# Ranking edges inside a tile by a summing comparison on VectorE: one sorting pass of a graph kernel, rebuilt

## The reference

```
# layer 0
att   = sigmoid(concat(h[src], rel[type]) @ att_w + att_b)      # one gate an edge
aggr  = segment_sum(att * h[dst], src)                          # by source node
x     = x + tanh(aggr @ W_w.T + W_b)
# layer 1: keys, values from h[dst], queries from h[src], weights from the attributes;
alpha = segment_softmax(sum(queries[src] * keys), src)
x     = x + lin(ssp(lin(h) + segment_sum(alpha * messages, src)))
```

## Time and profile before

| | |
|---|---|
| median of three runs | 7741.46 us (7740.86 to 7743.12) |
| the profiled execution | 7789.98 us, its span 7787.8 us, mean clock granted to TensorE 0.611 of full speed |
| busy over the span | PE 3233.5 us (42%), PEld 2600.9 (33%), VectorE 3605.5 (46%), ScalarE 2450.0 (31%), GpSimd 3252.3 (42%) |
| DMA | 497.92 MB, mean 64 GB/s |
| setup and histogram | up to about 283 us |
| sort | about 283 to 3963 us |
| layer 0 | to about 4600 us; layer 1 to about 7560 us |

### The profile page before, as it was taken

The page is one execution under the profiler, slowest core; times in us unless marked ns, Lnnn a source line. Parts: engine busy times, 40 slices in busy tenths (PEclk is TensorE's granted clock), DMA queues, the critical chain, the costliest instruction groups (busy, mean ns, idle before and its releaser), DMA issues. The chain is left out here.

```text
span 7787.8 us, 93760 instructions
## 1 busy us (share of the span) xinstructions
PE 3233.5 (42%) x31759; PEld 2600.9 (33%) x31760; DVE 3605.5 (46%) x6570; ACT 2450.0 (31%) x5029; POOL 3252.3 (42%) x3386
## 2 busy tenths in 40 slices
PE   4744444444444444444457743332222223332224
PEld 3633443343343343344357621111111111111113
DVE  7744443443444444444367724444444444444443
ACT  0122222222232232232212234444444444444432
POOL 0144344444434434434450045555555555555542
PEclk9866666666666666666666655555555555555555
DMA  3011111111111111111156322222333333333310
GB/s 46 29 52 45 42 50 45 43 49 46 44 42 52 45 42 52 45 42 51 37 126 125 76 75 83 83 83 83 86 86 86 88 84 84 84 84 83 86 55 17
DMA packets 651114, 497.92 MB, mean 64 GB/s; under 512 B 556547, under 2 KB 565379, under 8 KB 651056
## 3 DMA queue, kind: packets, MB, share of 16 engines
q1 hardware_dynamic: 509120, 240.52, 12.6%
q0 software_dynamic: 108640, 196.86, 8.7%
q10 hardware_dynamic: 33296, 59.81, 2.2%
HBM read 286.61 MB, written 210.32 MB: 64 GB/s over the span
## 5 line engine op out<-in xcount | busy, mean ns | idle before, releaser
L518 POOL DMA_INDIRECT records<-rec,place x1612 | 1550.5, 962 | 2388.8 <-ACTq L637 1901.1
L1210 POOL DMA_INDIRECT got_a<-kv_table,idx_a x1612 | 1524.3, 946 | 1418.5 <-DVE idx_a L1322 914.3
L1225 PE MATMUL p_a<-ident,flat_attr 128*128 128x128 f32 x434 | 124.3, 434 | 1730.6 <-ACT attr_t L1266 965.6
L550 PE MATMUL p_h<-window,dst_hot 128*128 128x64 bf16 x4836 | 378.2, 218 | 943.4 <-issue 943.4
L725 DVE TENSOR_SCALAR dst_hot<-p_dst,number 128x512 bf16<-128x512 f32 x434 | 308.9, 712 | 972.6 <-remote 707.4
L539 PE MATMUL p_look<-parts,lo_hot_t 128*128 128x98 bf16 x4836 | 538.1, 250 | 468.3 <-DVE earlier L743 461.2
L743 DVE TENSOR_TENSOR earlier<-p_same,less_b 128x512 bf16<-128x512 f32 x434 | 282.5, 651 | 938.7 <-PE p_same L585 519.7
L610 ACT COPY h_dst<-p_h 128x256 f32<-128x256 f32 x434 | 155.0, 357 | 1770.7 <-remote 1291.6
L1225 PEld LDWEIGHTS p_a<-ident,flat_attr 128*128 128x128 f32 x434 | 75.2, 214 | 1768.9 <-ACT attr_t L1266 989.9
L1345 DVE TENSOR_TENSOR prod<-got_a,wide 128x1664 f32<-128x1664 f32 x62 | 117.0, 1887 | 1108.8 <-remote 1107.7
L550 PEld LDWEIGHTS p_h<-window,dst_hot 128*128 128x128 bf16 x4836 | 280.5, 114 | 954.2 <-issue 954.2
(11 more groups left out here) (339 smaller groups left out, 9872.4 us busy)
## 6 DMA issues: line engine op xcount, KB each, us to landing
sums<-packed_a ACTq DMA_DIRECT2D x62, 936.0 KB
q_starts<-zero_q SPq DMA_DIRECT2D x62, 884.0 KB
rec_r<-records SPq DMA_DIRECT2D x124, 442.0 KB
qin<-q_starts SPq DMA_DIRECT2D x62, 884.0 KB
attr_a<-records SPq DMA_DIRECT2D x62, 442.0 KB
records<-rec,place POOLq DMA_INDIRECT x1612
got_a<-kv_table,idx_a POOLq DMA_INDIRECT x1612
stage<-in_edge_attr SPq DMA_DIRECT2D x61, 416.0 KB
```

Source lines behind the costliest of these rows:

```text
L518: nc.gpsimd.indirect_dma_start(k.records, bass.IndirectOffsetOnAxis(ap=place[b][:, t:t + 1], axis=0), rec[b][:, t, :], None).then_inc(s_se ...
L550: last = nc.tensor.matmul(p_h[:, j * D:(j + 1) * D], dst_hot[qb][:, j * P:(j + 1) * P], window[b][:, part, :], start=(part == 0), stop=(pa ...
L1210: nc.gpsimd.indirect_dma_start(got[b][:, t, :], None, k.kv_table, bass.IndirectOffsetOnAxis(ap=idx[b][:, t:t + 1], axis=0)).then_inc(s_got ...
L1225: last = nc.tensor.transpose(p_a[:, g * P - c0:(g + 1) * P - c0], flat_attr[:, g * G:(g + 1) * G, :].rearrange("p t c -> p (t c)"), k.iden ...
```

## The change

**Transposed one-hots without transposes.** `setup` writes three fields of all edges (lo, hi, and destination relative to the chunk) into DRAM (`field_rows`), each chunk's edges in a row by partition. SP loads a chunk's piece, three partitions of 3328 elements in bf16 (`fields`). TensorE reads a group's columns out of it with a step of 26 elements (`rows`) and multiplies them with `select`, three constant matrices of 3 x 128, in three products of 512 columns: p_lo repeats an edge's lo on all partitions, p_src its node number, p_dst its destination. ScalarE makes the transposed one-hots from p_lo by `relu(1 - |lo - partition|)`, an Abs into `lo_away` and a Relu into `lo_hot_t`, now in fp32.

**The rank in the tile on VectorE.** For each tile one `scalar_tensor_tensor` compares p_src with the edge's own source, multiplies by `before` (an earlier edge), and sums along the row into `rank`, an accumulator output. p_same, `earlier` and their product in `look` go.

**The places on VectorE.** p_place and its bf16 parts go. `tables` holds 52 tables of 49 numbers in fp32, one for each tile of two chunks, and the logit's behind them; VectorE adds a tile's counts from p_hist to a table to get the next (`add`, four a group). `look` is one fp32 product a tile, over the tile's table and the logit's, instead of three to seven in bf16. The place is summed with `rank` once a chunk (`s_place`).

**h in one part.** p_h is one fp32 product a tile, in one of two banks, from a window of `h_table`; `h3_table` goes, and `setup` no longer makes the three parts. ScalarE's gate products read p_h itself and write `h_gated`, so `h_copy` goes. `assemble` copies `h_gated` (1664 columns) and the gates into the record, and runs inside g == 2 instead of g == 3.

```
# setup, SP: ahead of the store of h_table
+   sp.wait_ge(s_fields, 1)
+   for a, field in enumerate((k.lo_b, k.hi_b, k.dst_in)):
+       sp.dma_start(k.field_rows[a, :].rearrange("(c p t) -> p c t", p=P, t=T),
+                    field[:].rearrange("p (c t) -> p c t", t=T)).then_inc(k.s_field_rows, 16)
    sp.dma_start(by_node(k.h_table), h[:]).then_inc(s_table, 16)
-   sp.dma_start(k.h3_table...)
# setup, VectorE
-   c.then(nc.vector.tensor_copy(h3[:, :, 0, :], h[:]))
-   c.then(nc.vector.tensor_tensor(h_rest[:], h[:], h3[:, :, 0, :], ALU.subtract))
-   c.then(nc.vector.tensor_copy(h3[:, :, 1, :], h_rest[:]))
-   nc.vector.tensor_tensor(h3[:, :, 2, :], h_rest[:], h3[:, :, 1, :], ALU.subtract).then_inc(s_h3, 1)
# sort, SP
+   wait(sp, s_dst, (n - 1) * GROUPS)
+   sp.dma_start(fields[b][:], k.field_rows[:, bass.ds(n * P * T, P * T)]).then_inc(s_fields[b], 16)
    wait(sp, s_h, (n - 1) * GROUPS)
-   sp.dma_start(window[b]..., k.h3_table[bass.ds(base, P), :])
+   sp.dma_start(window[b][:], k.h_table[bass.ds(base, P), :]).then_inc(s_window[b], 16)
# sort, GpSimd
+   pool.wait_ge(s_place, n + 1)
    pool.wait_ge(s_ready, n + 1)
# sort, TensorE: look(), for the group before
-   wait(pe, s_h_copied, q)
+   pe.wait_ge(s_tables, q + 1)
+   pe.wait_ge(s_lo_hot, q + 1)
    for j in range(size(g)):
+       last = nc.tensor.matmul(both, lo_hot_t[qb][:, j * P:(j + 1) * P], k.tables[:, slot:LOGIT + 1:LOGIT - slot, :], start=True, stop=True)
    ...
+   wait(pe, s_gated, q - 1)
+       last = nc.tensor.matmul(p_h[qb][:, j * D:(j + 1) * D], dst_hot[qb][:, j * P:(j + 1) * P], window[b][:], start=True, stop=True)
# sort, TensorE: a group
+   pe.wait_ge(s_fields[b], 16 * (i + 1))        # once a chunk
+   rows = fields[b][:].rearrange("r (p t) -> r t p", t=T)[:, g * G:g * G + m, :]
+   wait(pe, s_lo_away, q)
+   nc.tensor.matmul(p_lo[:, 0:m * P], k.select[:, LO, :], rows, start=True, stop=True).then_inc(s_lo, 1)
+   wait(pe, s_ranked, q)
+   nc.tensor.matmul(p_src[:, 0:m * P], k.select[:, NODE, :], rows, start=True, stop=True).then_inc(s_src, 1)
+   wait(pe, s_dst_hot, q)
+   nc.tensor.matmul(p_dst[:, 0:m * P], k.select[:, TO, :], rows, start=True, stop=True).then_inc(s_dst, 1)
+   wait(pe, s_tables, q)
    (counts into p_hist, then look of the group before)
-   (transposes, p_dst, p_same, p_place)
# sort, ScalarE
+   nc.scalar.activation(lo_away[qb][:, 0:m * P], p_lo[:, 0:m * P], ACT.Abs, bias=k.minus_number[:]).then_inc(s_lo_away, 1)
+   act.wait_ge(s_lo_away, q + 1)
+   wait(act, s_look, q - 1)
+   nc.scalar.activation(lo_hot_t[qb][:, 0:m * P], lo_away[qb][:, 0:m * P], ACT.Relu, bias=k.ones[:, 0:1], scale=-1.0).then_inc(s_lo_hot, 1)
    (gated:)
+   nc.scalar.activation(gate[b][:, ...], logit[b][:, ...], ACT.Sigmoid).then_inc(s_gate, 1)
+   for j, t in enumerate(tiles):
+       last = nc.scalar.activation(h_gated[b][:, t, :], p_h[qb][:, j * D:(j + 1) * D], ACT.Copy, scale=gate[b][:, t:t + 1])
+   last.then_inc(s_gated, 1)
    (assemble:)
-   nc.scalar.copy(place[b][:], place_all[:, cols])
+   wait(act, s_sent[b], SCATTERED * i)
+   nc.scalar.copy(rec[b][:, :, GATE], gate[b][:])
+   nc.scalar.copy(rec[b][:, :, H0:REC], h_gated[b][:])
-   if g == 3 and not at_start(i, b):
+   if g == 2 and not at_start(i, b):
        assemble(n - 1, i - 1 + b, 1 - b)
# sort, VectorE: a group
+   c.mark(add(b, g, 0))          # tables[slot + 1] = tables[slot] + p_hist of the tile
    dst_hot
+   c.wait(); c.mark(add(b, g, 1))
+   for j in range(m):
+       last = v.scalar_tensor_tensor(same_before[:, j, :], p_src[:, j * P:(j + 1) * P], k.src_f[:, bass.ds(n * T + t, 1)],
+                                     k.before[:], ALU.is_equal, ALU.mult, accum_out=rank[b][:, t:t + 1])
+   c.wait(); c.mark(add(b, g, 2))
    pick of two groups before
+   c.wait(); add(b, g, m - 1).then_inc(s_tables, 1)
    summed
    (one-hots if g == 3)
    logit of two groups before; at its last group:
+   v.tensor_tensor(place[b][:], place_gate[b][:, :, 0], rank[b][:], ALU.add).then_inc(s_place, 1)
-   (the parts of p_place, place_all, earlier)
```

More of the change, by code:

```diff
@@ L546, in look @@
                     pe.wait_ge(s_dst_hot, q + 1)
-                    wait(pe, s_h_copied, q)
+                    wait(pe, s_gated, q - 1)
                     for j in range(size(g)):
-                        for part in range(3):
-                            last = nc.tensor.matmul(p_h[:, j * D:(j + 1) * D], dst_hot[qb][:, j * P:(j + 1) * P], window[b][:, part, :],
-                                                    start=(part == 0), stop=(part == 2))
+                        last = nc.tensor.matmul(p_h[qb][:, j * D:(j + 1) * D], dst_hot[qb][:, j * P:(j + 1) * P], window[b][:], start=True, stop=True)
                     last.then_inc(s_h, 1)
@@ L717, in body @@
                             m = size(g)
[L718 to L722 removed]
+                            older = None if at_start(i, b) and g < 2 else behind(i, b, g)
+                            dve.wait_ge(s_hist, q + 1)
@@ L726, in body @@
+                            last.then_inc(s_ranked, 1)
+                            if m > 2:
+                                c.wait()
+                                c.mark(add(b, g, 2))
+                            if older:
+                                pick(older[0] * GROUPS + older[3], older[2], older[3], qb)
                             c.wait()
-                            c.mark(nc.vector.tensor_tensor(rest[:], p_place[:, 0:HI], parts[:, 0, :], ALU.subtract))
+                            add(b, g, m - 1).then_inc(s_tables, 1)
@@ L1700, in build @@
                 k.last_attr = tile("last_attr", [P, T, EC])
-                k.parts = [tile(f"parts{b}", [P, 3, 2, HI], BF16) for b in range(2)]
+                k.tables = tile("tables", [P, LOGIT + 1, HI])
                 setup(k)
```

246 lines of the change are left out of this document (103 added, 143 removed).

## The result

The changed kernel takes 7952.27 us (7946.61 to 7954.86, four runs) against 7742.29 us (7740.86 to 7744.05): 1.0268 of the kernel before, 95% interval 1.0255 to 1.028. It is slower, where I had forecast 7405 us with a range of 7130 to 7830. The profiled execution has a span of 7944.6 us, 156.8 more than before. GpSimd issues 26 x 49 = 1274 DMAs in the 3000 us in which it issued 1326, so a chunk has grown from 58.8 to 61.2 us. From the first indirect DMA to the last the pass takes 3764.4 us, where it took 3608.8: 156 us more. The first of them also goes 21 us later, and the stages behind the pass, whose code is the same, are 20 us shorter (3825.6 against 3845.3 us).

The account below looks back on a forecast made before the run. Bound: a chunk's slow part during GpSimd's indirect-DMA batch plus a quick part, 58.8 us. Chunks -324, setup -17 and assemble +3 from 7789.98 give 7452 us; scaled to the median, -336, the forecast is 7405 us, range 7130 to 7830.

Parts of the forecast that it names:

- about half, 2.7, at 2.4 GHz: TensorE in the sorting pass: a group of four tiles takes 5.2 us at 1.2 GHz, 2.7 at 2.4 GHz.
- the 4.4 us a group: Sorting pass outside the batch: full groups follow each other every 4.4 us, against 3.94 in the kernel before.
- the quick part: A chunk's stretch after GpSimd's batch of 26 indirect DMAs is drained: forecast 15.9 us, 20.4 before.
- the ring through ScalarE's gates: Sorting pass: wide product, Abs, Relu, sigmoid, gates and p_h wait for one another in a loop, 3.9 or 4.8 us.
- rival (b): Sorting pass: TensorE bounds, 6.5 us a group with slow stepped reads and low clock; chunk 61.2, kernel 7871 us; chance 0.20.
- the hold: Late signals of a batch: while GpSimd issues, TensorE's results are taken up 16 and 24 us late.
- How many groups a batch hides: Sorting pass: groups 3, 4 and 5 begin inside the batch, group 6 at 37.5 us; chunk 53.4 us instead of 58.8.
- 0.8 of a group of 23: In the batch's slow rest of some 27 us, 19 TensorE instructions come through, 0.8 of a group's 23.
- rival (a): The batch holds TensorE for a time, not by the instruction; group 5 waits until it drains: 7668 us; chance 0.15.
- the 7452 us of the sum: Whole kernel: profiled execution of 7789.98 us with -324 for the chunks, -17 for the setup, +3 for assemble.
- the estimate of 4.3 by that rule: VectorE's group takes 4.3 us if the comparing sums add four more small instructions of 0.12 us.
- The setup: Setup before the sorting pass: the histogram begins at 91 us instead of 109.6, -17 us; slow short pieces could lose it.

Follow-up runs that it names:

- look_twice: The changed kernel with every fp32 product of look issued twice: 8470.27 us, 1.0871 of the kernel before.
- contig: The changed kernel with the fields laid out by tile in DRAM, so wide products read 512 columns side by side: 7630.04 us, 0.9789 of the kernel before.
- h3_spaced: contig_h3 with GpSimd's indirect DMAs in parts of four, each waiting for a look, one look late: 6781.60 us, 0.8752 of the kernel before.
- wide_in_four: The changed kernel with each wide product cut into four of 128 columns: 8194.93 us, 1.0524 of the kernel before.
- contig_h3_again: contig_h3 unedited, run on a chip with the hold: 7490.77 us, 0.9672 of the kernel before.
- contig_h3: contig with h as three bf16 parts again, 12 products a group in p_h; chip without the hold: 5329.73 us, 0.9544 of the kernel before.
- after_again: The changed kernel unedited, run on a chip without the hold: 5907.70 us, 1.0579 of the kernel before.
- contig_again: contig unedited, run on a chip without the hold: 5468.58 us, 0.9792 of the kernel before.

## Why the prediction was wrong

**The step that failed is TensorE's time for a group at the full clock, "about half, 2.7, at 2.4 GHz", and with it the 4.4 us a group of the quick part.** A group takes 6.66 us at a granted clock of 1.00. I had taken TensorE's time as 5.2 us at the lower clock and 2.7 at the full one, and so let the ring through ScalarE's gates, 3.9 to 4.8 us, set the pace of the quick part. No product of this group got faster with the clock: the wide ones take the same at 0.50 and 1.00, with the step (look_twice, changed kernel) and without it (contig, h3_spaced), and look and p_h do too. So TensorE bounds at either clock, and the ring lies hidden beside it. Even by my own numbers it would have bounded at the lower clock, 5.2 against 4.8. Two terms are in the 6.66.

*The fp32 products.* 0.44 us each, read from rows at 0.50, was right to the second digit, but it is 0.44 at 1.00 too: 3.5 us a group, where I had halved it. contig at 0.50 and the changed kernel at 1.00 give the same 1.76 and 1.79. What doesn't shorten with the clock either is their weight load, 330 ns for 128 columns in fp32 at 1.00, and 330 in contig at 0.50, against 98 to 156 in bf16 (the weight loads by line and form, changed kernel; the mean is after the comma):

```profile
L540 PEld LDWEIGHTS p_h<-window,dst_hot 128*128 128x128 f32 x2539 | 576.1, 331 | 528.4 <-issue 525.6 <-DVE dst_hot L708 2.6
...
L561 PEld LDWEIGHTS p_hist<-hi_hot,lo_hot 128*128 128x128 bf16 x1270 | 114.0, 156 | 551.4 <-issue 512.5 <-DVE tables L661 38.8
...
L553 PEld LDWEIGHTS p_lo<-fields,select 3*128 3x128 bf16 x342 | 33.5, 98 | 40.3
```

That the load is the cause was only argued. The Trainium skill, "TensorE: Matmul & The Clock Gate", section "Weight-path perf modes — Fast Weight Load (FWL) and DoubleRow", says that the fast weight load is on for 128 weights when they are not fp32, and the rows agree in kind. The kernel's new stationary operands, `lo_hot_t` and `dst_hot`, are fp32 with 128 columns.

*The wide products.* I took 0.45 at the lower clock and half at the full one, and put the step of 26 elements into rival (b). Side by side they take 0.40 to 0.42, so the 0.45 was near without the step, and the halving wrong; with the step they take 0.87. The step is 3 x 0.45 = 1.35 us a group. contig, which takes it away and also begins the histogram 27 us sooner, is 4.7% faster than the changed kernel with the hold and 7.4% without (5468.58 against 5907.70 us). The Trainium skill, "SBUF — State Buffer", section "Door 1: The DMA port swizzle (why `[64,N]` ≈ `[32,N]`)", has a rule for this, though no price: accesses run at full rate while they stay on the same line of 16 bytes, and each one that goes to a new line pays, so bf16 may be read with a step of up to 8 elements for free. At 26 elements, 52 bytes, each read is on a new line, and the traces agree: 1.7 ns a column, against 0.8 side by side.

**How many groups a batch hides** was wrong as well. I had groups 3, 4 and 5 begin inside, and group 6 at 37.5 us. In the runs groups 3 and 4 do, group 5 begins at 36.2 and group 6 at 40.1. The step in words is the rounding of "0.8 of a group of 23" to a whole one, but the picture behind it, instructions that trickle at a fixed rate from 5 us on, was wrong too. From 1966.8 to 1981.2 TensorE's timeline has nine of a group's 23 instructions, 0.63 a us, where I had taken 0.69; up to 1966.8, 19 us into the batch, it runs at its full pace. What group 5 waits for is not issue but a signal: its counts are issued at 1964.41, and VectorE takes them up at 1981.21.

```profile
1964.80 1.97 PE L533 MATMUL p_look<-tables,lo_hot_t 128*128 128x98 f32 x8
1973.40 1.94 PE L540 MATMUL p_h<-window,dst_hot 128*128 128x64 f32 x8 [6.64 <-issue]
1975.28 0.60 PE L553 MATMUL p_lo<-fields,select 3*128 3x256 bf16 x1
```

This is rival (a)'s case: group 5 begins only when the batch is drained. Whether for its reason, a hold purely by time, is open: wide_in_four speaks against it, with the doubt named there, and contig_h3_again for it.

So group 6 begins at 40.1 us and not at 37.5, and the way from it to the next batch, 15.9 us by the prediction, is 21.4: 6.6 to group 0, 4.95 to group 1, 6.66 to group 2, 3.2 to the batch. Rival (b) came true in its size. Its 6.5 us a group is right term by term (3.5 for the fp32 products, 0.4 for the counts, 2.6 for the wide ones; measured 3.55, 0.39, 2.72), though its condition, that the clock stays low, did not hold and did not matter. Its point of decision, 5.8 us a group, fits the runs: contig, with 5.3, is faster than the kernel before, and 6.66 is slower. That its chunk of 61.2 us is the measured one to the digit is in part luck, 37.5 + 23.7 where the trace has 40.1 + 21.4.

The profiled execution misses the 7452 us of the sum by 495. The pass has 480 of them, the setup 22, and 16 are a term that I left out: nothing hides the longer groups of the first chunk. Against them stand 3 us of my own that I had added and the 20 us of the unchanged stages.

**What held.** The p_dst signal is late in the batch. The one-hots lie inside it. A comparing sum starts 0.27 us after the last, where I took 0.28, and VectorE's group, where it waits for nobody, is 3.81 us, where I had 3.8. The Trainium skill, "VectorE: DVE Perf Modes", section "Two Vector instructions with no wait between them", has the accumulator read as an instruction of its own, and the trace agrees (its row has the same count as the sums'). But its 83 ns lie beside the next sum, so the estimate of 4.3 by that rule was too high. assemble's long copy is 1.58 us, where I had 1.75. Abs and Relu are 0.69 and 0.72, above my 0.58, and hidden.

**The setup** was forecast at -17 us and measured at +5.2. The term was the stores of short pieces. SP issues the three in 29.9 us where I had 25, and the store of h_table behind them, 0.40 us to issue in the kernel before, takes 18.07; the histogram's first instruction stands behind 28.2 us of an idle VectorE. I had named this ("up to all of it is lost"), but not that it could be more than all.

**What the loss is.** Without the hold the sum is plain: TensorE needs 43.4 us a chunk, and GpSimd's batch with its hand-over, which had bounded with 38.3, is no longer the longest. With the hold the same 6.66 us a group stand in the quick part. The rank on VectorE is not what made the kernel slower: outside the drain its sums are hidden, and the fp32 look, the fp32 p_h and the step are. Taking away two of the three (contig_h3) turns 1.058 into 0.954.

**Open.** What the hold is. The runs show that it comes while GpSimd issues indirect DMAs and shrinks when GpSimd pauses, that it begins some 5 us into a batch in the kernel before and after more than 12.9 us in contig, that it ends with the batch or up to 4 us behind it, and that some chips have none. In the stretches read here it is TensorE's signals that come late. Which bytes or which unit TensorE's signals queue behind, no run shows. Whether SP's burst at the start of a batch, or pauses by GpSimd's own work, move it was not tried on a chip that has it.

## What to carry to other kernels

Fewer instructions is not less time: count TensorE's time for a group from rows of the same type and the same step, and don't halve a product's time because the clock is full before a row at that clock shows it; here neither the fp32 products nor the wide ones got faster. A moving operand read with a step of 52 bytes costs twice what one side by side does; lay it out once, ahead of the loop. Where a long batch of indirect DMAs bounds or holds up others, let it pause in step with the work: on the chips with the hold that alone was worth 7 to 12%, more than any change of the arithmetic here, and on the others contig lost nothing by it.

## What the runs showed of the hardware that I had not expected

The same program takes 7742 us on one chip and 5586 on another. Between the two traces of it lie 2204 us. 1240 are in the sort's pass (3609 against 2369 us from the first indirect DMA to the last), where the late signals are; 963 lie in the stages behind (3845 against 2882), which this study did not take apart. fp32 products of 64 to 98 columns take 0.22 us for each of their two instructions at a granted clock of 0.50 and of 1.00 alike. The wide products keep theirs too: 0.87 us with the step at 0.51 and 1.00, 0.40 to 0.42 without it at 0.50 and 1.00. Nor does the step decide what clock is granted: look_twice has it and 0.51, h3_spaced lacks it and has 1.00. Without the hold the changed kernel was granted 1.00 (after_again, busy 2000 of 2000 us) and contig 0.50 (contig_again, busy 1929.89 of 2000):

```profile
400.00:2400.00 2000.00, 1929.89 (x8245) 1470.29 (x8245) 1466.10 (x5954) 1028.94 (x2836) 1426.07 (x1422) 0.50 0.23 74
```

contig's time for a group was the shorter all the same.
